# Audio tower layer in fp32: first-pass feed-forward blocks 4 to 15 as three fp32r products, some weights' low parts from accumulating DMAs

## The reference, cut to what matters

```python
h = patches(x) @ W.T + b                              # 64 x 10 x 512
h = h + attention(layernorm(h), Wq, Wk, Wv, Wo)
h = h + ffn(layernorm(h), w_gate_up, w_down)

def ffn(x, w_gate_up, w_down):
    gate, up = split(x @ w_gate_up.T, 2)              # 512 -> 2 x 2048
    return (silu(gate) * up) @ w_down.T               # 2048 -> 512
```

## Time and profile before

| | us |
|---|---|
| median of 3 runs | 285.42 (284.55 to 286.07) |
| the profiled execution, whole | 284.75 |
| the profiled execution, its span | 282.8 |
| of it: first pass, from block 2 to the start of the second | 83.3 to 175.6 |
| of it: second pass and results | 175.6 to 282.8 |

### The profile page before, as it was taken

One profiled execution on the slowest core, in us unless ns is written; L12 is line 12 of the kernel. 1 busy time (PEld: TensorE's weight loads), 2 busy tenths in 40 slices (PEclk: granted clock), 3 DMA queues, 4 the chain that ended last, 5 costly groups with the idle time before them and its releaser, 6 DMA issues.

```text
span 282.8 us, 4587 instructions
## 1 busy us (share of the span) xinstructions
PE 273.1 (97%) x1781; PEld 215.7 (76%) x1781; DVE 161.6 (57%) x312; ACT 79.5 (28%) x148; POOL 53.0 (19%) x41
## 2 busy tenths in 40 slices
PE   7999999999799999999999999999999999999994
PEld 6555486683687867767865667899999999999992
DVE  1676998995779998669704535453333443333313
ACT  2311214520510112350101123243344443433330
POOL 0104000010024510007300001052222223322210
PEclk9999999999999999999999999999999999999999
DMA  7994030000005334534403023385444333330003
GB/s 229 416 415 135 1 114 2 2 2 0 1 16 197 124 114 127 205 113 148 188 0 111 23 92 121 127 312 184 135 137 167 117 111 111 111 111 0 0 0 111
DMA packets 6815, 32.76 MB, mean 116 GB/s; under 512 B 976, under 2 KB 976, under 8 KB 6288
## 3 DMA queue, kind: packets, MB, share of 16 engines
q1 hardware_dynamic: 6512, 32.15, 32.4%
q10 hardware_dynamic: 288, 0.39, 0.4%
HBM read 31.23 MB, written 1.31 MB: 115 GB/s over the span
## 4 chain that ended last, share of the span: by engine, by line
PE 93%; DVE 2%; ACT 2%; issue 1%; POOL 0%; DVEq 0%; POOLq 0%
PE ps L210 36%; PE ps L1075 18%; PE ps L1085 10%; PE ps L952 5%; PE ps L1014 5%; PE ps L1006 4%; PE ps L930 4%; PE ps L967 3%; PE ps L957 3%; PE ps L883 2%; PE ps L1019 1%; PE ps L936 1%; PE ps L994 1%; ACT v_all L395 1%; PE ps L887 1%
## 5 line engine op out<-in xcount | busy, mean ns | idle before, releaser
L210 PE MATMUL ps<-xT,wgu 128*128 128x384 f32 x384 | 70.9, 340 | 0.1
L210 PEld LDWEIGHTS ps<-xT,wgu 128*128 128x128 f32 x384 | 68.1, 188 | 2.5 <-DVE xT L577 0.9
L1075 PE MATMUL ps<-whole,stage 128*128 128x256 f32 (+1 forms) x288 | 58.3, 357 | 1.0 <-ACT whole L362 1.0
L1075 PEld LDWEIGHTS ps<-whole,stage 128*128 128x128 f32 x288 | 49.6, 190 | 11.7 <-issue 4.8
L790 DVE TENSOR_TENSOR gu<-silu,ps 128x256 f32<-128x256 f32 (+1 forms) x32 | 15.5, 484 | 67.7 <-PE ps L210 44.8
L303 POOL TENSOR_TENSOR wd<-stage,wd 128x512 fp32r<-128x512 f32 x16 | 26.8, 1675 | 78.7 <-ACT wd L362 78.7
L210 PE MATMUL ps<-wd,hT 128*128 128x512 f32 x144 | 35.7, 393 | 0.0
L467 ACT ACTIVATE silu<-ps 128x256 f32<-128x256 f32 (+1 forms) x32 | 14.0, 438 | 75.0 <-PE ps L1075 48.6
L210 PEld LDWEIGHTS ps<-wd,hT 128*128 128x128 f32 x144 | 26.8, 188 | 5.0
L1085 PE MATMUL ps<-stage,gu 128*128 128x512 f32 x64 | 30.1, 592 | 0.0
L362 ACT ACTIVATE wgu<-stage 128x1024 fp32r<-128x1024 f32 x16 | 16.9, 1058 | 22.6 <-PE ps L210 20.9
(11 more groups left out here) (100 smaller groups left out, 252.0 us busy)
## 6 DMA issues: line engine op xcount, KB each, us to landing
stage<-w_ffn SPq DMA_DIRECT2D x32, 768.0 KB, 4.3
stage<-w_k SPq DMA_DIRECT2D x1, 1024.0 KB, 6.7
stage<-w_q SPq DMA_DIRECT2D x1, 1024.0 KB, 10.1
stage<-w_v SPq DMA_DIRECT2D x1, 1024.0 KB, 12.2
wo<-w_o SPq DMA_DIRECT2D x1, 1024.0 KB, 13.8
out<-ob SPq DMA_DIRECT2D x14, 64.0 KB, 2.3
const<-consts SPq DMA_DIRECT2D x1, 800.0 KB, 8.1
out<-ob ACTq DMA_DIRECT2D x6, 64.0 KB, 1.9
```

What stands on the lines that cost most here:

```text
L210: ins = pe.matmul(dst, lhs[a], rhs[b], start=first and n == 0, stop=last and n == 2)
L1075: ins = pe.matmul(ps[:, bank, at + a:at + b], stage[:, slot, w:w + P], xf[:, k, a:b], start=k == 0, stop=k == KT - 1)
```

## The change

Three constants are new: blocks 4 to 15 (`S1` = 4) take gate and up as three fp32r products, and blocks 11 to 15 (`S0` = 11, `NS` = 5) take down so too.

- The tokens of tiles 0 and 1 are split once into high and low parts `xs` (`hi_whole` on ScalarE, `low_whole` on VectorE).
- For blocks 4 to 10 ScalarE writes minus the weights into the low place of `wgu` and the rounded weights into the high place; a DMA, issued by GpSimd, then adds the weights of `stage` to what stands in the low place (`low_weights`, 512 KB each). Both copies are rounded to fp32r, so that the sum is the weight less its rounded value, the low part.
- For blocks 11 to 15 ScalarE makes the high parts of both weights (`hi_weights`), VectorE the low ones (`low_weights`), and `hT` is split on ScalarE and VectorE (`low_units`).
- ScalarE's and VectorE's lists are written in a new order, and the second pass's counts are shifted by five.

```diff
+NS = 5
+S0 = NB - NS
+S1 = 4
...
+            def low_weights(i):
+
+                pool.wait_ge(minus_set, i - S1 + 1)
+                pool.dma_start(wgu[:, i % 2, 1], stage[:, i % SLOTS, 0:2 * KT * P], accum_op=ALU.add).then_inc(low_sum[i % 2], 16)
...
+            def minus_weights(i):
+
+                slot, ring = i % SLOTS, i % 2
+                act.wait_ge(dma_stage[slot], stage_count(A, i, slot))
+                if i >= S1 + 2:
+                    act.wait_ge(gu_mm[A], 2 * (i - 1))
+                act.activation(wgu[:, ring, 1], stage[:, slot, 0:2 * KT * P], ACT.Copy, scale=-1.0)
+                act.activation(wgu[:, ring, 0], stage[:, slot, 0:2 * KT * P], ACT.Copy).then_inc(minus_set, 1)
+
+            def hi_weights(i):
+
+                slot, ring = i % SLOTS, i % 2
+                act.wait_ge(dma_stage[slot], stage_count(A, i, slot))
+                act.wait_ge(gu_mm[A], 2 * (i - 1))
+                split_hi(wgu[:, ring, 0], stage[:, slot, 0:2 * KT * P], wgu_hi)
+                if i >= S0 + 2:
+                    act.wait_ge(down_mm[A], i - 1)
+                hi_down(i, ring, slot)
...
             def first_pass(i):
                 silu_gate(A, i, i % 2)
+                if i >= S0:
+                    act.wait_ge(gu_prod[A], i + 1)
+                    split_hi(hT[:, i % 2, 0, 0:2 * P], gu[:, i % 2, 0:2 * P], hT_hi)
...
+            def low_weights(i):
+
+                slot, ring = i % SLOTS, i % 2
+                lo_gu(i - NB, ring, slot)
+                dve.wait_ge(wd_hi, i - S0 + 1)
+                dve.tensor_tensor(wd[:, ring, 1], stage[:, slot, 2 * KT * P:FW], f32(wd[:, ring, 0]), ALU.subtract).then_inc(wd_lo, 1)
+
+            def low_units(i):
+
+                dve.wait_ge(hT_hi, i - S0 + 1)
+                dve.tensor_tensor(hT[:, i % 2, 1, 0:2 * P], gu[:, i % 2, 0:2 * P], f32(hT[:, i % 2, 0, 0:2 * P]), ALU.subtract)\
+                   .then_inc(hT_lo, 1)
...
+                if i >= S1:
+                    pe.wait_ge(xs_lo, 1)
+                    if i >= S0:
+                        pe.wait_ge(wgu_lo, i - S0 + 1)
+                    else:
+                        pe.wait_ge(low_sum[i % 2], 16 * ((i - S1) // 2 + 1))
...
+                if i >= S0:
+                    pe.wait_ge(hT_lo, i - S0 + 1)
+                    pe.wait_ge(wd_lo, i - S0 + 1)
+                else:
+                    pe.wait_ge(gu_prod[A], i + 1)
...
             first_pass(12)
+            low_units(12)
             statistics(LN2[2])
             normalise(LN2[2])
+            low_weights(14)
             statistics(LN2[4])
             first_pass(13)
```

More of the change, by code:

```diff
@@ L346, in _ @@
             values(0, 8)
+            low_weights(4)
             scores(1, 5)
+            low_weights(5)
             scores(1, 7)
+            for i in range(6, S0):
+                low_weights(i)
             values(1, 8)
@@ L486, in second_pass @@
                         act.wait_ge(down_mm[Z], i)
-                        act.wait_ge(wd_lo, i)
+                        act.wait_ge(wd_lo, i + NS)
                     hi_down(i + 1, 1 - ring, (u + 1) % SLOTS)
-            for i in range(4):
+            first_pass(0)
+            hi_whole()
+            first_pass(1)
+            first_pass(2)
+            minus_weights(4)
+            first_pass(3)
+            minus_weights(5)
+            hi_attn(2)
+            for i in range(4, 8):
                 first_pass(i)
-            hi_attn(2)
-            for i in range(4, 7):
-                first_pass(i)
+                minus_weights(i + 2)
             exponential(4)
-            for i in range(7, 9):
-                first_pass(i)
+            first_pass(8)
+            minus_weights(10)
+            first_pass(9)
+            hi_weights(11)
+            first_pass(10)
             exponential(5)
-            for i in range(9, 12):
-                first_pass(i)
+            hi_weights(12)
+            first_pass(11)
             hi_attn(3)
             hi_attn(4)
+            hi_weights(13)
             first_pass(12)
@@ L505, in _ @@
             hi_xT(LN2[2])
+            hi_weights(14)
             first_pass(13)
             hi_xT(LN2[4])
+            hi_weights(15)
             first_pass(14)
@@ L511, in _ @@
             first_pass(15)
+            act.wait_ge(down_mm[A], NB - 1)
             hi_down(0, 0, 0)
@@ L821, in _ @@
             scores(1, 3)
+            low_whole()
             turn("q", 1)
@@ L861, in _ @@
             first_pass(15)
+            low_units(15)
             lo_gu(1, 1, 1)
@@ L1069, in gate_up_whole @@
                 slot, ring = i % SLOTS, i % 2
+                a, b = P * tiles[0], P * tiles[-1] + P
+                if i >= S1:
[4 more added lines that the diff above has]
+                        pe.wait_ge(low_sum[i % 2], 16 * ((i - S1) // 2 + 1))
+                    for up, (bank, at) in enumerate((GATE[A][ring], UP[A][ring])):
+                        for k in range(KT):
+                            w = D * up + P * k
+                            ins = mm3(pe, ps[:, bank, at + a:at + b], [wgu[:, ring, n, w:w + P] for n in range(2)],
+                                      [xs[:, n, k] for n in range(2)], k == 0, k == KT - 1)
+                        ins.then_inc(gu_mm[A], 1)
+                    return
                 pe.wait_ge(dma_stage[slot], stage_count(A, i, slot))
-                a, b = P * tiles[0], P * tiles[-1] + P
                 for bank, at in (GATE[A][ring], UP[A][ring]):
@@ L1098, in gate_up @@
             def gate_up(i, ring):
-                pe.wait_ge(wgu_lo, i + 1)
+                pe.wait_ge(wgu_lo, i + (NS + 1))
                 for up, (bank, col) in enumerate((GATE[Z][ring], UP[Z][ring])):
```

60 lines of the change are left out of this document (39 added, 21 removed).

## The result

The changed kernel takes 309.26 us (median of 4, 305.26 to 311.01) against 285.47 us (median of 4, 284.55 to 286.07): 23.8 us slower. The ratio of 1.075 (95% interval 1.065 to 1.085) is that of its two shorter executions, 305.26 and 308.24 us with a median of 306.75, because the two longer ones count as slow by their lower granted clock, though here a lower clock is part of what the change does. The prediction was 297.5 us, at most 306.8: the median of all four lies above that range, that of the two shorter ones at its very edge. It had the sign and half of the size.

What follows compares the result with a forecast made beforehand. TensorE, busy 97%, was taken to bound the kernel. Savings of 6.8 us against 19.3 us of waits, less 0.33 from down(15), gave +12.1 on 284.75, 296.8, and 0.67 to the median: 297.5 us, range 290.5 to 306.8.

Steps and rivals of the forecast that it cites:

- the clock: TensorE's granted clock, 1.00 before; its fall behind a wait was named as a sign of error, with no time given.
- D: Blocks 4 to 10: time from ScalarE's last copy to the accumulating DMA's landing, issue included, taken as 5.0 us.
- TensorE's own work: Blocks 4 to 15: cheaper matmuls at 0.125 us per 256 columns, saving 7.1 us if TensorE never waits.
- Rival B: Gate and up: 256-column matmuls at 0.177 us, with the same waits +19.7, 305.1 us; chance 7%.
- 19.3 us of waits: Up to the second pass: 7.85 for weights, 3.35 attention, 7.65 layer norms and 0.45 before the second pass.
- The accumulating DMA: Blocks 4 to 10: TensorE waits for landings of 2.85, 1.1, 1.0, 0.1 and 2.3 us in blocks 5 and 7 to 10.
- Rival C: Slow accumulate, D at 6.5 us or more, by shared engines or GpSimd's issue: 302.0 us at 6.5; chance 20%.
- Block 11: Its low part stands behind first_pass(10) on VectorE, so TensorE waits 0.5 us.
- The attention stretch: VectorE's low parts of blocks 11 and 12 and a late softmax delay the value sums: 3.35 us of waits.
- The layer norms: Blocks 12 to 15: weight splitting delays statistics and normalise, so transposes wait 1.5, 2.8 and 3.3 us, sum 7.65.
- the 0.45 before the second pass: Just ahead of the second pass, product 15 is late: 0.45 us of wait.
- Rival A: Whole kernel faster, waits summing to less than 7.1 us, 278.3 us if fully covered; chance 9% for over 0.5% faster.

Runs made afterwards that it cites:

- e6: e1 with the layer norms put first in ScalarE's and VectorE's lists (down-weight parts later, statistics and normalise earlier): 289.45 us, ratio 1.015.
- e3: The changed kernel with extra fp32 matmuls whose results nobody reads, put ahead of TensorE's waits: 303.04 us, ratio 1.063.
- e4: The changed kernel with its seven accumulating DMAs copying instead of adding, so the low parts are wrong: 300.11 us, ratio 1.053.
- e9: e1 with the lists reordered for layer norms and attention, up to block 10 as in the kernel before, block 15's low parts earlier: 282.66 us.
- e12: The whole change with all accumulates, in e9's orders and with block 5's DMA ahead of the scores: 290.49 us, ratio 1.016.
- e5: The changed kernel with the loads of blocks 8 and 10 cut from 768 to 64 KB, most of their weights missing: 308.62 us, ratio 1.082.
- e1: The changed kernel with only blocks 11 to 15 changed; blocks 4 to 10 stay fp32 without accumulating DMAs: 297.89 us, ratio 1.046.
- e8: The changed kernel with block 5's accumulating DMA issued ahead of the product for scores (1, 5) on GpSimd: 306.76 us.

## Why the prediction was wrong

**The step that failed is the clock: the sum had no term for it, and the slower groups cost 9.9 us. The second is the size of the accumulates that meet a load (7.1 to 7.9 us where D was 5.0).** The second pass began at 201.4 us and not at 188. The terms in the order of the prediction:

**TensorE's own work: right mechanism, size off to the good side.** A 256-column matmul costs 2.82/24 = 0.1175 us after a wait, and a step of gate, up and down goes from 5.17 to 4.46 us (108.33 to 112.79), so 0.7 us less and not 0.45. Down is 1.38 us, as predicted. I had 6.8 us saved up to the second pass; it is 9.4. Rival B (0.177) falls. Its sum was wrong too: with the same 19.3 us of waits, a pitch of 0.177 gives about +27 us and not +19.7, beyond my range. By the Trainium skill, "TensorE: Matmul & The Clock Gate", section "Back-to-back issue gap", the estimate was 109 ns; the trace's 117.5 lies 8.5 above it, my 125 lay 7.5 above the trace.

**The accumulating DMA: D was right for one that no load precedes closely, under-sized right behind a load.** From the last copy's end to the landing it was 5.0 us in block 8 and 4.8 in block 10, my value, but 7.9, 7.1 and 7.3 us in blocks 6, 7 and 9. Rival C had the mechanism, packets that share engines with stage loads, and I gave it 20% because I took the 0.44 busy share as an average that every transfer meets. It is 0.97 in the stretch at 103.8 and the loads are triggered by the very step that triggers the accumulate. The waits were 2.96 (predicted 2.85), 3.42 and 3.55 us in blocks 5, 7 and 9 instead of 2.85, 1.1 and 0.1, and none in 8 and 10 where I had 1.0 and 2.3: 9.9 in place of 7.35. That the sum came so near is partly luck: the longer waits of blocks 7 and 9 gave blocks 8 and 10 the cover that I had not counted. I had also put later block loads at nothing; the copies of block 8 waited 2.15 us for theirs, though TensorE did not wait for it. By the formula of the Trainium skill, "DMA: Bandwidth & Descriptors", section "Anatomy of one DMA — SWDGE (gpsimd) path", the estimate for both reads was 4.4 us. The trace agrees within half a microsecond where no load went out in the 3 us before (4.5 to 4.8 us), and not right behind a load.

**Block 11: right** (0.54 against 0.5 us).

**The attention stretch: under-sized**, 4.60 us in place of 3.35. VectorE's timeline:

```profile
150.10 2.99 DVE L833 TENSOR_TENSOR wgu<-stage,wgu 128x1024 fp32r<-128x1024 f32 x1
153.01 1.78 DVE L857 TENSOR_TENSOR wd<-stage,wd 128x512 fp32r<-128x512 f32 x1
```

These two fell beside the three `values` on GpSimd (7.62 us from 146.63) and took 4.8 us, where I had put 1.7 from rows without such a neighbour. The rows that I read for their price did not contain their company.

**The layer norms: right.** 1.75, 2.91 and 3.52 us against 1.5, 2.8 and 3.3, and e6 shows that the order of the lists is the cause. For the last tile VectorE shows the chain link by link:

```profile
192.96 0.69 DVE L857 TENSOR_TENSOR wd<-stage,wd 128x512 fp32r<-128x512 f32 x1 [3.01 <-ACT wd L376]
...
196.50 0.42 DVE L862 TENSOR_TENSOR hT<-gu,hT 128x256 fp32r<-128x256 f32 x1 [0.48 <-ACT hT L376]
196.85 0.68 DVE L631 TENSOR_TENSOR xT<-ps,xT 128x512 fp32r<-128x512 f32 x1
...
198.00 0.55 DVE L619 TENSOR_SCALAR xn<-h,mv,rstd 128x512 f32<-128x512 f32 x1
```

From the end of down(13) at 192.09 to the end of xn at 198.55 are 6.5 us, predicted 6.2.

**The clock: the step that failed.** I wrote that I am wrong "if the granted clock falls behind a wait" and gave it no price. The trace of before could not show it, since TensorE never waited there; but I had predicted waits of 2.85, 2.8 and 3.3 us on an engine that had had none. It costs 9.9 us of slower groups in the profiled execution, 6.2 us of the median or 3.7 us by the two shorter executions (e3). With the clock kept up the kernel takes 303.04 us, inside my range and 5.5 us above the forecast. The account of the miss up to the second pass, 25.1 against 12.4 us: 9.9 the clock, 3.9 more waiting (2.6 at DMAs, 1.25 at values, 0.5 at norms, less the 0.45 before the second pass, which the slow group ahead of it hid: e4, whose clock is up there, waits 0.41), 1.4 around the waits, less 2.6 saved by the shorter pitch.

**Rival A, faster,** needed waits below 7.1 us and had 23.2. For the last five blocks the orders decide: e9 is on the faster side. For the whole change they are not enough: e12, in the same orders, is still slower than the kernel before.

Open is what decides whether the clock falls behind a wait. It fell at one of 2.25 us (e5, 121.6 us) and stayed at 1.00 behind ones of 2.62 and 3.52 us (e4). The wait of 2.91 us at the transposes had a fall behind it in the changed kernel and none in e1, e4 and e8. So the length of the wait alone does not tell. No run here separates the other causes, and the last 1.3 us of e12 were not pursued.

## What to carry to other kernels

Cheaper matmuls leave less cover for the engines that feed them. Price each new wait twice, once for its length and once for the clock behind it, and give that second term a number in the sum even where the trace before has no such wait. A conversion of weights belongs behind the operations for which the bound engine waits next; the same work in another order was 15 us apart (e1 and e9). For a DMA that must land in time, look at what else its trigger sets off: a transfer priced alone will meet the load that the same step releases.

## What the runs showed of the hardware

- TensorE's clock went to its low level at six waits of 2.9 us or more of one execution, four times before the wait was over, and stayed there for 3.4 us (6.8 once). Filling the waits with matmuls that nobody reads kept the mean clock at 0.997 to 1.000, against 0.961 to 0.983, and gained 6.2 us by the medians, 3.7 against the two shorter executions (e3).
- An accumulating DMA of 512 KB within the on-chip memory took 4.5 to 4.8 us from issue to landing where no load of 768 KB went out in the 3 us before it, and 6.8 to 7.6 us within 0.9 us behind one. Over the other runs such a close load went with 5.7 to 8.6 us. A plain copy of the same size took 2.9 to 3.8 us in four of seven cases, 4.5 in one, and 5.3 and 7.3 within 1 us behind a load (e4). The load goes from 4.3 to as much as 5.8 us. The issue takes 0.87 us on GpSimd, against 0.54 for the plain one.
- VectorE's subtraction of 1024 columns takes 1.22 us and 2.99 beside GpSimd's products; its product of 400 columns 0.57 and 2.30 beside a subtraction on GpSimd.
